# A quantised feed-forward stage: the rounding step from a ScalarE square, the input's chain moved from GpSimd to VectorE

## The reference

```python
def fp4_quant_dequant(x):                     # BLOCK = 16
    scale = jnp.max(jnp.abs(xb), axis=-1, keepdims=True) / 6.0
    scale = jnp.maximum(scale, jnp.float32(1e-12))
    xn = xb / scale
    idx = jnp.searchsorted(_MID, jnp.abs(xn))
    q = _GRID[idx] * jnp.sign(xn) * scale     # _GRID 0, 0.5, 1, 1.5, 2, 3, 4, 6
gate = fp4_linear(x, w_gate)                  # 128 -> 352, both operands rounded
y = fp4_linear(x, w_up)
h = jax.nn.silu(gate) * y
return fp4_linear(h, w_down)                  # 352 -> 128
```

## Time and profile before

| | |
|---|---|
| median of 3 runs | 4230.71 us (4229.49 to 4238.97) |
| profiled execution, its span from first to last instruction | 4250.5 us |
| mean granted TensorE clock | 0.817 |
| PE / DVE / ACT / POOL busy in the span | 68% / 65% / 40% / 48% |
| stage l2fa, first scale to last residual | 175.2 us |
| stage l3fb, the same | 176.1 us |

### The profile page before, as it was taken

One profiled execution on the slowest core, in us unless ns is written; L12 is line 12 of the kernel. 1 busy time (PEld: TensorE's weight loads), 2 busy tenths in 40 slices (PEclk: granted clock), 3 DMA queues, 4 the chain that ended last, 5 costly groups with the idle time before them and its releaser, 6 DMA issues. The chain is left out here.

```text
span 4250.5 us, 64084 instructions
## 1 busy us (share of the span) xinstructions
PE 2877.9 (68%) x22097; PEld 1782.5 (42%) x22097; DVE 2748.4 (65%) x5884; ACT 1703.2 (40%) x2994; POOL 2032.5 (48%) x2683
## 2 busy tenths in 40 slices
PE   5848367775493659659488746687565888467846
PEld 3748312221493338449233334233243333244534
DVE  4634468884344852343588669688497887595678
ACT  2413147675131314334265612466422566224511
POOL 6643332210433222232365467355595564585686
PEclk9869669997597759869699868799786999686967
DMA  5113132210121012002212000222001221000000
GB/s 166 42 54 90 38 104 81 81 56 27 57 87 50 0 50 72 19 19 67 75 70 84 32 1 0 89 72 84 2 1 46 76 77 47 0 1 1 1 0 20
DMA packets 217155, 206.14 MB, mean 48 GB/s; under 512 B 49432, under 2 KB 194008, under 8 KB 216073
## 3 DMA queue, kind: packets, MB, share of 16 engines
q1 hardware_dynamic: 204552, 176.85, 12.9%
q0 software_dynamic: 12288, 25.19, 1.9%
HBM read 103.55 MB, written 96.47 MB: 47 GB/s over the span
## 5 line engine op out<-in xcount | busy, mean ns | idle before, releaser
L979 DVE TENSOR_REDUCE l0b_negm<-l0b_ps_s 128x2 f32<-128x1024 f32 x256 | 304.2, 1220 | 50.7 <-PE l0b_ps_s L732 49.7
L822 ACT ACTIVATE l0b_E<-l0b_ps_t 128x1024 f32<-128x1024 f32 x256 | 262.0, 1023 | 132.4 <-PE l0b_ps_t L714 132.2
L822 ACT ACTIVATE l2a_E<-l2a_ps_t 128x768 f32<-128x768 f32 (+1 forms) x192 | 169.4, 882 | 134.0 <-PE l2a_ps_t L714 133.2
L822 ACT ACTIVATE l3a_E<-l3a_ps_t 128x768 f32<-128x768 f32 (+1 forms) x192 | 169.4, 882 | 127.6 <-PE l3a_ps_t L714 126.7
L979 DVE TENSOR_REDUCE l2b_negm<-l2b_ps_s 128x2 f32<-128x256 f32 (+3 forms) x256 | 196.4, 818 | 27.5 <-PE l2b_ps_s L737 27.3
L822 ACT ACTIVATE l2b_E<-l2b_ps_t 128x768 f32<-128x768 f32 (+1 forms) x192 | 169.3, 882 | 106.6 <-PE l2b_ps_t L714 105.8
L979 DVE TENSOR_REDUCE l3a_negm<-l3a_ps_s 128x2 f32<-128x256 f32 (+3 forms) x256 | 196.3, 819 | 17.1 <-PE l3a_ps_s L737 17.0
L979 DVE TENSOR_REDUCE l2a_negm<-l2a_ps_s 128x2 f32<-128x256 f32 (+3 forms) x256 | 196.0, 818 | 17.3 <-PE l2a_ps_s L737 17.2
L899 POOL TENSOR_SCALAR_AFFINE_SELECT l2b_E<-l2b_E 128x256 f32<-128x256 f32 x256 | 100.7, 409 | 177.3 <-ACT l2b_E L822 177.3
L899 POOL TENSOR_SCALAR_AFFINE_SELECT l2a_E<-l2a_E 128x256 f32<-128x256 f32 x256 | 101.5, 409 | 170.8 <-ACT l2a_E L822 169.0
L899 POOL TENSOR_SCALAR_AFFINE_SELECT l3a_E<-l3a_E 128x256 f32<-128x256 f32 x256 | 101.6, 409 | 163.4 <-ACT l3a_E L822 161.5
(11 more groups left out here) (985 smaller groups left out, 9083.3 us busy)
## 6 DMA issues: line engine op xcount, KB each, us to landing
room_up<-l0b_stack SPq DMA_DIRECT2D x32, 192.0 KB
room_down<-l0b_stack SPq DMA_DIRECT2D x32, 192.0 KB
room_up<-l2a_stack SPq DMA_DIRECT2D x32, 192.0 KB
room_down<-l2a_stack SPq DMA_DIRECT2D x32, 192.0 KB
room_up<-l2b_stack SPq DMA_DIRECT2D x32, 192.0 KB
room_down<-l2b_stack SPq DMA_DIRECT2D x32, 192.0 KB
room_up<-l3a_stack SPq DMA_DIRECT2D x32, 192.0 KB
room_down<-l3a_stack SPq DMA_DIRECT2D x32, 192.0 KB
```

What stands on the lines that cost most here:

```text
L822: act.activation(probs(n % 3, c, 0)[:, 2 * p:2 * p + 2, :], ps_t[:, :, 0:width[c]], ACT.Exp, scale=scale).then_inc(probs_ready.sem, 1)
L979: e = dve.tensor_reduce(negm[:, qt, :, j], ps_s[n % 2][:, :, off:off + keys[qt]], AX.X, ALU.max, negate=True)
```

## The change

In the four stages GpSimd gets no work. The large number that sets the rounding is now GRID_BASE + square: ScalarE squares the divided value with a factor (`steps_x(u)` for the input, `squares(u)` for h), so that the sum passes a power of two where the value passes 2.12 and 3.97. VectorE adds and takes off that sum with one SCALAR_TENSOR_TENSOR each, (square + GRID_BASE) + v and v - (square + GRID_BASE), so the two operations that made the number on VectorE, and the five on GpSimd, are gone. The input's division, rounding and multiplication go to VectorE (`divide_x(u)`, `round_x(u)`). quantize_h is split into `divide_h(u)` up to v and `round_h(u)`. The input's side now runs four steps ahead, the products three, h's division one; before it was two, one and none. v, scale, x_v and the squares have two buffers. A small constant, grid_base, is made at the start of the program.

The diff, cut to the order and the new calls:

```diff
+    core.grid_base = core.sb("grid_base", [P, 1])
...
+GRID_BASE = 1.2 * 2.0 ** 22
+GRID_SCALE = math.sqrt(0.8 * 2.0 ** 22) / 2.12
...
-        @block.gpsimd
-        def _(pool):
-            ch = Chain(pool_step, pool, 0)
-
-            def quantize_x(u):
...
+        def half(u):
+            return slice(u % 2 * NX, (u % 2 + 1) * NX)
 
         @block.vector
         def _(dve):
@@ -3198,18 +3183,45 @@
                 ch.link(dve.reciprocal(i, sc))
                 dve.tensor_scalar(i, i, 1.0 - 2.0 ** -23, None, ALU.mult).then_inc(x_inv_ready.sem, 1)
 
-            def multiply(u, t):
-                dve.wait_ge(act_ready.sem, act_ready.upto(u * T2 + t + 1))
-                dve.tensor_tensor(h[:, t, :], sg[t][:, :], ps_g[t][:, 1, 0:HID], ALU.mult).then_inc(mul_done.sem, 1)
-
-            def quantize_h(u):
+            def divide_x(u):
+                if u >= 2:
+                    dve.wait_ge(xq_ready.sem, xq_ready.upto(u - 1))
+                dve.wait_ge(x_inv_ready.sem, x_inv_ready.upto(u // 2 + 1))
+                dve.tensor_tensor(x_v[u % 2][:, :, :], blocks(x_tiles(u)), wide(x_inv[u // 2 % 2][:, half(u)], NX),
+                                  ALU.mult).then_inc(x_v_ready.sem, 1)
+
+            def round_x(u):
+                dve.wait_ge(x_step_ready.sem, x_step_ready.upto(u + 1))
+                if u >= 2:
+                    dve.wait_ge(xqT_in_psum.sem, xqT_in_psum.upto(u - 1))
+                x, q = x_v[u % 2][:, :, :], x_step[u % 2][:, :, :]
+                ch.link(dve.scalar_tensor_tensor(x, q, GRID_BASE, x, ALU.add, ALU.add))
+                ch.link(dve.scalar_tensor_tensor(x, q, GRID_BASE, x, ALU.add, ALU.subtract, reverse1=True))
+                dve.tensor_tensor(blocks(xq[u % 2][:, :, :]), x, wide(x_scale[u // 2 % 2][:, half(u)], NX),
+                                  ALU.mult).then_inc(xq_ready.sem, 1)
+
+            def multiply(u):
+                for t in range(T2):
+                    dve.wait_ge(act_ready.sem, act_ready.upto(u * T2 + t + 1))
+                    dve.tensor_tensor(h[:, t, :], sg[t][:, :], ps_g[t][:, 1, 0:HID], ALU.mult).then_inc(mul_done.sem, 1)
+
+            def divide_h(u):
                 dve.wait_ge(mul_done.sem, mul_done.upto((u + 1) * T2))
-                if u >= 1:
-                    dve.wait_ge(quant_ready.sem, quant_ready.upto(u))
+                sc, i = scale[u % 2][:, :], inv[:, :]
+                ch.link(dve.tensor_reduce(sc, blocks(h[:, :, :]), AX.X, ALU.max, apply_absolute_value=True))
+                ch.link(dve.tensor_scalar(sc, sc, 1.0 / 6.0, 1e-12, ALU.mult, ALU.max))
+                ch.link(dve.reciprocal(i, sc))
+                ch.link(dve.tensor_scalar(i, i, 1.0 - 2.0 ** -23, None, ALU.mult))
+                dve.tensor_tensor(v[u % 2][:, :, :], blocks(h[:, :, :]), wide(i, NH), ALU.mult).then_inc(v_ready.sem, 1)
+
+            def round_h(u):
+                dve.wait_ge(squares_ready.sem, squares_ready.upto(u + 1))
                 if u >= 2:
                     dve.wait_ge(quantT_in_psum.sem, quantT_in_psum.upto(2 * (u - 1)))
-                quantize(ch, dve, blocks(hq[u % 2][:, :, :]), blocks(h[:, :, :]), v[:, :, :], power[:, :, :], scale[:, :],
-                         inv[:, :]).then_inc(quant_ready.sem, 1)
+                x, q = v[u % 2][:, :, :], square[u % 2][:, :, :]
+                ch.link(dve.scalar_tensor_tensor(x, q, GRID_BASE, x, ALU.add, ALU.add))
+                ch.link(dve.scalar_tensor_tensor(x, q, GRID_BASE, x, ALU.add, ALU.subtract, reverse1=True))
+                dve.tensor_tensor(blocks(hq[u % 2][:, :, :]), x, wide(scale[u % 2][:, :], NH), ALU.mult).then_inc(quant_ready.sem, 1)
 
             def add(u):
                 x = core.X[:, u * T2:(u + 1) * T2, :]
@@ -3218,12 +3230,26 @@
 
             scales_x(0)
             scales_x(1)
+            divide_x(0)
+            divide_x(1)
+            for u in range(4):
+                round_x(u)
+                divide_x(u + 2)
+                if u % 2 == 1:
+                    scales_x(u // 2 + 2)
+            multiply(0)
+            divide_h(0)
             for u in range(ALL):
-                for t in range(T2):
-                    multiply(u, t)
-                if u % 2 == 1 and u // 2 + 2 < B:
-                    scales_x(u // 2 + 2)
-                quantize_h(u)
+                if u + 1 < ALL:
+                    multiply(u + 1)
+                    divide_h(u + 1)
+                if u + 4 < ALL:
+                    round_x(u + 4)
+                if u % 2 == 1 and u // 2 + 4 < B:
+                    scales_x(u // 2 + 4)
+                if u + 6 < ALL:
+                    divide_x(u + 6)
+                round_h(u)
                 if u >= 1:
                     add(u - 1)
             add(ALL - 1)
...
-            transpose_x(0)
-            input_products(0)
-            transpose_x(1)
+            for u in range(3):
+                transpose_x(u)
+                input_products(u)
+            transpose_x(3)
             for u in range(ALL):
-                if u + 1 < ALL:
-                    input_products(u + 1)
-                if u + 2 < ALL:
-                    transpose_x(u + 2)
                 transpose_h(u)
+                if u + 3 < ALL:
+                    input_products(u + 3)
                 output_products(u)
+                if u + 4 < ALL:
+                    transpose_x(u + 4)
 
         @block.scalar
         def _(act):
+            def steps_x(u):
+
+                act.wait_ge(x_v_ready.sem, x_v_ready.upto(u + 1))
+                act.activation(x_step[u % 2][:, :, :], x_v[u % 2][:, :, :], ACT.Square, scale=GRID_SCALE).then_inc(x_step_ready.sem, 1)
+
+            def squares(u):
+                act.wait_ge(v_ready.sem, v_ready.upto(u + 1))
+                act.activation(square[u % 2][:, :, :], v[u % 2][:, :, :], ACT.Square, scale=GRID_SCALE).then_inc(squares_ready.sem, 1)
+
...
+            steps_x(0)
+            steps_x(1)
             read_xT(0)
             gates(0)
+            steps_x(2)
             read_xT(1)
+            steps_x(3)
+            squares(0)
+            gates(1)
+            read_xT(2)
+            squares(1)
+            gates(2)
             for u in range(ALL):
-                if u + 1 < ALL:
-                    gates(u + 1)
+                if u + 4 < ALL:
+                    steps_x(u + 4)
+                if u + 3 < ALL:
+                    read_xT(u + 3)
+                read_hT(u)
                 if u + 2 < ALL:
-                    read_xT(u + 2)
-                read_hT(u)
+                    squares(u + 2)
+                if u + 3 < ALL:
+                    gates(u + 3)
```

More of the change, by code:

```diff
@@ L148 @@
     "row_mean_ready",
+    "x_v_ready",
+    "x_step_ready",
     "row_stats_ready",
@@ L277, in _ @@
             pool.memset(core.onesb[:, :], 1.0).then_inc(made, 1)
+            pool.memset(core.grid_base[:, :], GRID_BASE).then_inc(made, 1)
             pool.memset(core.earlier[:, :], 1.0).then_inc(made, 1)
@@ L280, in _ @@
             pool.tensor_scalar(core.rank8[:, :], core.iota8[:, :], -1.0, 8.0, ALU.mult, ALU.add).then_inc(made, 1)
-            pool.wait_ge(made, 30)
+            pool.wait_ge(made, 31)
             pool.affine_select(out=core.earlier[:, :], in_=core.earlier[:, :], compare_op=ALU.is_gt, fill=0.0, base=0,
@@ L286, in _ @@
             pool.memset(core.pick_rows[:, :, :], 0.0).then_inc(made, 1)
-            pool.wait_ge(made, 33)
+            pool.wait_ge(made, 34)
             for k in range(3):
@@ L291, in _ @@
                                    pattern=[[-1, B], [0, P]], channel_multiplier=1).then_inc(made, 1)
-            pool.wait_ge(made, 36)
+            pool.wait_ge(made, 37)
 def store_stage(core, out):
@@ L3118, in quantized_ffn_stage @@
     W = T2 * P
-    MAGIC = 0.75 * 2.0 ** 23
     with ExitStack() as ctx:
@@ L3128, in quantized_ffn_stage @@
         x_inv = [sb(f"x_inv{u}", [P, 2 * NX]) for u in range(2)]
-        x_v = sb("x_v", [P, NX, BLOCK])
-        x_square = sb("x_square", [P, NX, BLOCK])
-        x_power = sb("x_power", [P, NX, BLOCK])
+        x_v = [sb(f"x_v{u}", [P, NX, BLOCK]) for u in range(2)]
+        x_step = [sb(f"x_step{u}", [P, NX, BLOCK]) for u in range(2)]
         xq = [sb(f"xq{u}", [P, T2, D]) for u in range(2)]
@@ L3135, in quantized_ffn_stage @@
         h = sb("h", [P, T2, HID])
-        scale = sb("scale", [P, NH])
+        scale = [sb(f"scale{u}", [P, NH]) for u in range(2)]
         inv = sb("inv", [P, NH])
-        v = sb("v", [P, NH, BLOCK])
-        power = sb("power", [P, NH, BLOCK])
+        v = [sb(f"v{u}", [P, NH, BLOCK]) for u in range(2)]
+        square = [sb(f"square{u}", [P, NH, BLOCK]) for u in range(2)]
         hq = [sb(f"hq{u}", [P, T2, HID]) for u in range(2)]
@@ L3145, in quantized_ffn_stage @@
         ps_o = psum("ps_o", [P, T2, D])
[L3146 to L3149, removed]
+        sig = core.begin(dve_step=1, x_inv_ready=1, x_v_ready=1, x_step_ready=1, xq_ready=1, xqT_in_psum=1, xT_ready=1,
```

(31 more changed lines are left out.)

## The result

The changed kernel takes 4269.24 us (median of 4 runs, 4268.01 to 4273.1) beside 4233.33 for the kernel before (4 runs, 4229.49 to 4238.97): ratio 1.0086, 95% interval 1.007 to 1.0101. It is slower by 36 us, where 32 were forecast. The profiled execution took 4268.01 us, its span is 4266.3. That is only 15.8 us above the span before, since the profiled execution before reached l2fa 24 us later (at 2482.3 against 2458.2; at 2456.5 in a second profile of it). So the kernels are compared by their medians, and the profiles stage by stage.

What follows compares the result with a forecast made beforehand. VectorE was taken to bound the four feed-forward stages, GpSimd close behind. Each stage was to grow 8.0 us, from 176.1 to 184.1, four of them 32, so 4230.7 + 32 = 4263 us; range 4222 to 4305.

Steps and rivals of the forecast that it cites:

- The bound and the relief: Feed-forward stages: VectorE bounds them; with GpSimd silent its 128x704 operations take 0.89 us, against a median of 1.296.
- Work of a step: VectorE's work in one step of a stage, everything but the scales of x: 8.39 us.
- The wait: VectorE before round_x, held by ScalarE's square, gates and x step: 1.91 to 2.46 us a step, mean 2.18.
- The start: Start of a stage: RX(2) stops 3.0 us behind the first gates; M(0), the first gate multiplication, at 16.65.
- The end: Steps 12 and 13 at 6.73 us each, two outputs in sequence at 5.08, 1.0 added for slow TensorE; stage 184.1.
- The stages together: Four feed-forward stages: each 184.1 us against 176.1, 8.0 more, together 32 us.
- The step that failed: Rest of the program outside the four stages: grid_base nobody waits long for, weights' quantisation unchanged, 0.
- VectorE's busy time: VectorE in each feed-forward stage: busy time falls to about 146 us while the stage grows to 184.
- the first: Rival: wait before round_x doesn't show, only relief from GpSimd counts; 105 us less in all, 4158; chance 0.12.
- the second's three terms: Rival, wait and relief cancel: wait 1.91, last two outputs fast, nothing for TensorE in steps 12 to 14; 4231; chance 0.12.
- The slow one: Rival: TensorE slow through the stage, wait 2.46, SCALAR_TENSOR_TENSOR 0.05 dearer; 10.6 us a stage, 4305; chance 0.15.
- table loads between them: Rival: Square and Silu displace each other's ScalarE table, two 1.283 us loads per wait; 31 us a stage, 4386; chance 0.01.

Runs made afterwards that it cites:

- two others: Changed kernel with round_h(u) moved between divide_h(u+1) and round_x(u+4): 4161.31 us; changed kernel with ScalarE's x step one step earlier, ahead of square and gates: 4161.57 us.
- the last two runs: Changed kernel with l3fa put back as before: 4267.28 us, mixer 230.0; kernel before with only l3fa changed: 4236.79 us, mixer 225.9.

## Why the prediction came out as it did

- **The bound and the relief** were right. VectorE bounds the stage; without GpSimd its 128x704 operations stand at 0.89. The SCALAR_TENSOR_TENSOR was priced like a TENSOR_TENSOR: 0.884 and 0.892. The Square was put at 0.79 and took 0.790, the 256-wide operations at 0.42.
- **Work of a step**, 8.39: a step of 10.27 us with a wait of 1.87 in it leaves 8.40. One of 11.18 with 2.78 leaves 8.40 too.
- **The wait**, 2.18: the 12 take 26.7 us, 2.23 each. The low end of 1.91 was right for seven of them, 1.86 or 1.87. Of the other five, two took 2.09 and 2.10, and three, 2.78, 3.18 and 3.50, went over the high end of 2.46 (its terms as written give 2.42). It was sized too low: the slow products were put at 4.02 us and took 4.49 and 4.89 in those three steps (granted clock 0.52 in the step shown), so the gate waited longer. That the fewer slow steps and their higher price cancelled in the mean is luck.
- **The start**: M(0) at 16.8 behind the stage's start (16.65 forecast), the first stop 3.32 (3.0).
- **The end**: steps 12 and 13 take 6.60 each (6.73), and the 1.0 us set aside for a slow TensorE there didn't occur. Slow products did, once (4.03 us from 4227.85), but with transposes of 1.14 and an output of 1.50 TensorE kept pace. The two outputs one after the other came as forecast; the second wait was 4.31 in l3fb and 2.7 or 2.8 in the three others, where the last output took 1.60 us (granted clock 1.00 in l3fa) against 2.93 in l3fb (0.50). These stages took 182.0 to 182.7, and l3fb 183.7, where 184.1 had been worked out.
- **The stages together**: +27.0 in place of +32. The sum was sized on the last stage, the one that grew most (7.6 us, the others 6.0 to 6.8), and multiplied by four.
- **The step that failed is one that the sum left out**: everything beside the four stages stood at nothing. That rest holds 10.8 us in the mixer, nearly a third of the difference, and it more than made up for the 5 us too many in the stages. So the forecast of 4263 is nearer than its terms were, and that too is luck. No run shows what would have let the mixer be forecast.
- **VectorE's busy time** was put at about 146 us without working; it is 139.5.
- **The rivals**: the first was wrong for this order and right for two others, at 4161 and 4162 where I had written 4158; there the stages gained more than it says (77 and 82 us, not 73), and the mixer took 5 and 11 back. Of the second's three terms the last held (nothing for TensorE near the end), the wait of 1.91 held in seven of 12 steps, and the fast outputs for one of two in three stages. The slow one, with the SCALAR_TENSOR_TENSOR dearer, didn't occur. Nor did table loads between them: two gates and a Square follow each other above with no gap.

## What to carry to other kernels

An operation that waits belongs behind work of its own engine that is ready. Before a chain is split between two engines, write both queues side by side and look for the loop in which each asks for what the other will do last; here moving one call turned +0.9% into -1.8% with the same instructions. A cheaper chain and a relieved port are worth nothing while such a wait takes more than they save, so look at the waits and not at the busy time.

## What the runs showed of the hardware

GpSimd's contention with VectorE was known from the trace, its size was not. The 131 us of GpSimd work added in each stage cost VectorE 18 to 21 us there (busy 157.2 to 160.4 in place of 139.5), though nothing waited for them.

The mixer's time depends on which program it is in: 225.9, 227.1 and 227.5, 230.0, 232.9 twice, 237.7 to 238.4 in four programs, and the two programs that were profiled twice gave their own value again. In all twelve profiles it goes with the granted clock of TensorE. In the window from 80 to 100 us behind l3fa's end that stood at 0.97 to 1.00 where the mixer took 225.9 to 227.5, at 0.91 or 0.92 where it took 230.0 to 232.9, and at 0.77 to 0.79 where it took 237.7 to 238.4. A difference of 10 us in a stage that a change doesn't touch is thus no scatter and not the change's own work either. What decides when the clock rises there is open: the last two runs speak against the end of l3fa by itself and against the program as a whole, and other causes weren't tried.
